# Reading and inverting most softmax denominators before two attentions end, and a reordered ScalarE loop in the first projection

## The chip, the cores and the metric

One core of a Trainium2 chip runs the whole program: TensorE (PE, matrix products), VectorE (DVE), ScalarE (ACT), GpSimd (POOL) and SyncE (SP, which here only issues DMAs). Each engine follows its own instruction list, and they meet through semaphores. The metric is the device time of one execution in microseconds, lower is better.

## The reference

The program is four layers over 8 sequences of 512 tokens with 128 features. Each layer adds an attention-like stage and then a mixture of experts. Only two stages are touched, the attentions of layers 0 and 1. Both have 16 heads of 8 features. Cut to what matters:

```python
# layer 0: 16 query heads, 8 key heads, and a memory read beside the attention
scores = einsum('bsnd,btnd->bnst', q4, k4) * scale
a_dot = einsum('bnst,btnd->bsnd', softmax(scores), v4)
a_mem = (elu(q) @ memory) / (elu(q) @ memory_norm)[..., None]
x = x + a_dot * (1 - w) + a_mem * w
# layer 1: the same with 16 key heads and a causal mask; q, k, v come from three "pattentions"
o = causal_sdpa(q, k, v)
```

The 8 sequences are called chunks here (NB = 8, L = 512 columns each, x is kept transposed as 128 features by 4096 tokens).

## The kernel before

The stages a0 (layer 0's attention), f0 (its experts), a1, f1, a2 and so on follow each other. Each stage is one or more blocks: an instruction list per engine, with a barrier of all engines between two blocks, so a block starts when the last engine has left the one before.

**The projection of layer 0** (`layer0_project`) loops over the chunks. Per chunk PE makes denominators and numerators of the memory read, projects q, k and v of the chunk two ahead, counts squares of up to three weight tiles ("jobs": the weight norms of f0, 17 jobs in all, spread over chunks 1 to 6; `count_squares`), and then spreads the inverted denominators over the rows (`spread_inverse`, L1366). ACT per chunk moves q, k and v out of PSUM with their variants, squares the job tiles (L1447, which wait in turn for PE to have counted earlier jobs), copies the numerators of the chunk before (`copy_num`, L1411) and widens its inverted denominators (`widen`, L1417). PE's `spread_inverse` of that chunk waits for `widen`.

**The attention** (`attend`) works a chunk at a time in 8 waves, half of a chunk behind its own score tiles (BEHIND = 4). For every group of 4 heads the maxima go through a short chain: DVE reduces, POOL splits them in three parts, PE turns them, DVE copies them to SBUF, POOL stores the 12 KB rows to DRAM (L1040), waits for them to land, and loads them back as rows of the operand `a_q` (L1043); the score products of that group wait for this. The products with v, whose 9th row of each head is the softmax denominator, are evacuated by ACT (L1164) and stored by SP as `a_pv_rows` (L947), 256 KB per group of 4 heads. Two operand buffers alternate: chunk 6 uses buffer 0, chunk 7 buffer 1. SP's block ends after the last store has landed.

**The division** (`combine`, a block of its own after the attention) loads all 128 denominator rows (L1557), inverts them on DVE (L1584), builds a 0/1 matrix `a_pick` on POOL (L1566, L1569), and for each chunk spreads the inverses with one f32 product of PE (L1579, two MATMUL instructions) and multiplies the numerators with them (L1590 in layer 1; L1592 and L1595, which also weighs and adds into x, in layer 0). The numerators are loaded 256 KB at a time into four buffers (L1561).

Of the kernel before, what the change touches and what calls it, by code (L numbers as in the profile page):

```python
# [12 lines left out]
F32 = mybir.dt.float32  # L13
# [850 lines left out]
def attend(nc, S, a):  # L864
# [7 lines left out]
    s, KVH, HK = S.at, a.KVH, H // a.KVH  # L872
    call = s.calls
    s.calls += 1
    with ExitStack() as ctx:
# [61 lines left out]
        def _(sp):  # L937
# [44 lines left out]
            for b in range(1, NB):  # L982
                body(b, True, True, b % 2)
            body(NB, False, True, 0)
            for k in range(2):
                sp.wait_ge(s.pv_stored[k], 16 * 2 * (nB + NB))

        @block.gpsimd
        def _(pool):
# [56 lines left out]
            steps(pool, body)  # L1046

# [133 lines left out]
        def _(dve):  # L1181
# [25 lines left out]
            steps(dve, body)  # L1207
    if a.causal:
        s.causal += 1
# [34 lines left out]
def layer0_attention(nc, S, inp, f):  # L1244
# [23 lines left out]
    attend(nc, S, a)  # L1268
    held.close()
    combine(nc, S, a, S.x, S.w_dot[:, 0:1])  # L1270


def layer0_project(nc, S, a, w, f):
# [19 lines left out]
    def jobs_of(c):  # L1293

        return range(min(3 * (c - 1), JOBS), min(3 * c, JOBS)) if c >= 1 else range(0)

    with ExitStack() as ctx:
# [105 lines left out]
        def _(act):  # L1403
# [16 lines left out]
            for c in range(NB):  # L1420
# [119 lines left out]

def combine(nc, S, a, dst, weight=None):

    sem, nm = S.sem, a.name
    den_loaded, inverse, picked = sem(f"{nm}_den_loaded"), sem(f"{nm}_inverse"), sem(f"{nm}_picked")
    num_loaded = [sem(f"{nm}_num_loaded{k}") for k in range(4)]
    spread, multiplied = sem(f"{nm}_spread"), sem(f"{nm}_multiplied")
    with ExitStack() as ctx:
        num = ctx.enter_context(nc.sbuf_tensor(f"{nm}_num", [P, 4, L], F32))
        den = ctx.enter_context(nc.sbuf_tensor(f"{nm}_den", [P, L], F32))
        pick = ctx.enter_context(nc.sbuf_tensor(f"{nm}_pick", [P, NB, P], F32))  # L1550
        inv = ctx.enter_context(nc.psum_tensor(f"{nm}_inv", [P, 4, L], F32))
        rows = a.pv.rearrange("b g (j r) n -> (b g j) r n", j=4)
        block = ctx.enter_context(nc.Block())

        @block.sync
        def _(sp):
            sp.dma_start(den[:, :], rows[:, DH, :]).then_inc(den_loaded, 16)  # L1557
            for b in range(NB):
                if b >= 4:
                    sp.wait_ge(multiplied, b - 3)  # L1560
                sp.dma_start(num[:, b % 4, :], rows[H * b:H * b + H, 0:DH, :]).then_inc(num_loaded[b % 4], 16)  # L1561

        @block.gpsimd
        def _(pool):

            nc.gpsimd.memset(pick[:, :, :], 0.0).then_inc(picked, 1)  # L1566
            pool.wait_ge(picked, 1)
            view = pick[:, :, :].rearrange("k b (h d) -> k (b h) d", d=DH)
            nc.gpsimd.affine_select(out=view, in_=view, compare_op=ALU.not_equal, fill=1.0, base=0,  # L1569
                                    pattern=[[-1, P], [0, DH]], channel_multiplier=1).then_inc(picked, 1)  # L1570

        @block.tensor
        def _(pe):
            pe.wait_ge(picked, 2)
            pe.wait_ge(inverse, 1)
            for b in range(NB):
                if b >= 4:
                    pe.wait_ge(multiplied, b - 3)
                nc.tensor.matmul(inv[:, b % 4, :], pick[:, b, :], den[:, :], start=True, stop=True).then_inc(spread, 1)  # L1579

        @block.vector
        def _(dve):
            dve.wait_ge(den_loaded, 16)
            nc.vector.reciprocal(den[:, :], den[:, :]).then_inc(inverse, 1)  # L1584
            for b in range(NB):
                dve.wait_ge(num_loaded[b % 4], 16 * (b // 4 + 1))
                dve.wait_ge(spread, b + 1)
                to = dst[:, b * L:(b + 1) * L]
                if weight is None:
                    nc.vector.tensor_tensor(to, num[:, b % 4, :], inv[:, b % 4, :], ALU.mult).then_inc(multiplied, 1)  # L1590
                else:
                    nc.vector.tensor_tensor(num[:, b % 4, :], num[:, b % 4, :], inv[:, b % 4, :], ALU.mult  # L1592
                                            ).then_inc(inverse, 1)
                    dve.wait_ge(inverse, b + 2)
                    nc.vector.scalar_tensor_tensor(out=to, in0=num[:, b % 4, :], scalar=weight, in1=to,  # L1595
                                                   op0=ALU.mult, op1=ALU.add).then_inc(multiplied, 1)
# [271 lines left out]
def layer1_attention(nc, S, inp):  # L1868
# [3 lines left out]
    with ExitStack() as ctx:  # L1872
# [23 lines left out]
        attend(nc, S, a)  # L1896
        held.close()
        combine(nc, S, a, g)
# [1144 lines left out]
```

## Time and profile before

| | us |
|---|---|
| median of 3 runs (lowest to highest) | 3603.91 (3601.78 to 3606.88) |
| the profiled execution | 3613.86 |
| its span, first to last instruction | 3612.1 |
| PE busy | 3240.8 (90% of the span) |
| DVE busy | 2450.0 (68%) |
| ACT busy | 1820.7 (50%) |
| POOL busy | 1191.2 (33%) |
| mean granted PE clock, as a share of 2.4 GHz | 0.926 |

The profile is of one execution that took 3613.86 us. Its span leaves out 1.8 us around the first and the last instruction. Busy shares are means over stages that have different limits, so the change is read in the three short stretches that it touches.

### The profile page before, as it was taken

What the parts mean: (1) busy time and instruction counts of PE and PEld (TensorE: products, weight loads), DVE (VectorE), ACT (ScalarE), POOL (GpSimd) and SP (SyncE); (2) the same over time, 40 slices, a digit from 0 to 9 for tenths busy, and PEclk for the clock granted to TensorE, in tenths of its full rate; (3) what the DMA queues carried; (4) which work ended last, traced back from release to release, by engine and by line L of the source; (5) the groups of instructions that cost most, each with busy time, mean ns of one, the idle gap of its engine ahead of it and who ended that gap; (6) DMA issues with size and microseconds to landing.
All of it is one profiled execution on the core that took longest, in us unless ns stands there. A gap on an engine that the chain in (4) does not pass through costs nothing. (4 is left out here: it accounts for less than half of the span.)

```text
span 3612.1 us, 39566 instructions
## 1 busy us (share of the span) xinstructions
PE 3240.8 (90%) x12845; PEld 1536.3 (43%) x12845; DVE 2450.0 (68%) x4164; ACT 1820.7 (50%) x2881; POOL 1191.2 (33%) x1010
## 2 busy tenths in 40 slices
PE   8899998999997699979998789898898789889999
PEld 5422224444444354535544233333333354764443
DVE  4788874443338577746544899999999955656544
ACT  5366672444446355534333777777777633312221
POOL 4211110000002222210000799999999910210000
PEclk7699998999998799989899899999999979889999
DMA  4222201000002533110000443443443410000000
GB/s 129 66 69 65 61 31 33 1 0 1 1 19 81 132 88 91 60 39 1 1 1 25 153 153 147 148 157 144 155 152 147 147 45 3 1 1 1 0 1 24
DMA packets 113335, 232.14 MB, mean 64 GB/s; under 512 B 27701, under 2 KB 82378, under 8 KB 95754
## 3 DMA queue, kind: packets, MB, share of 16 engines
q1 hardware_dynamic: 109034, 228.02, 19.0%
q0 software_dynamic: 4096, 1.59, 0.2%
q8 instruction: 104, 1.70, 0.2%
q14 instruction: 101, 0.83, 0.1%
HBM read 191.46 MB, written 34.87 MB: 63 GB/s over the span
## 5 line engine op out<-in xcount | busy, mean ns | idle before, releaser
L1199 DVE TENSOR_REDUCE a_top<-a_sc 128x1 f32<-128x512 f32 (+3 forms) x1024 | 547.2, 584 | 162.3 <-PE a_sc L1075 102.5
L2406 POOL TENSOR_TENSOR a_g<-a_g,a_spread 128x1024 f32<-128x1024 f32 x255 | 597.7, 2363 | 41.4 <-DVE a_g L2336 40.8
L2336 DVE TENSOR_TENSOR_SCAN a_g<-a_decay,a_drive 128x512 f32<-128x512 f32 x510 | 587.1, 1201 | 16.3 <-ACT a_drive L2225 12.9
L1156 ACT ACTIVATE a_prob<-a_st 128x1024 f32<-128x1024 f32 (+2 forms) x512 | 422.5, 862 | 280.7 <-PE a_st L1092 182.9
L705 DVE TENSOR_TENSOR f_s<-f_a,f_spread 128x512 f32<-128x512 f32 x392 | 269.4, 687 | 381.8 <-PE f_y L547 170.6
L2084 PE MATMUL a_y<-a_g,ident 128*128 128x512 f32 x1024 | 481.0, 610 | 31.3 <-POOL a_g L2406 31.3
L538 PE MATMUL f_hid<-h,f_w 128*128 128x512 f32 x784 | 404.2, 597 | 0.0
L547 PE MATMUL f_y<-f_s,f_w 128*128 128x512 f32 x784 | 401.6, 594 | 2.6 <-DVE f_s L705 2.6
L2209 ACT ACTIVATE a_decay<-a_delta,a_capped_a 128x512 f32<-128x512 f32 x512 | 331.8, 710 | 12.4 <-DVE a_g L2336 9.7
L1072 PE MATMUL a_sc<-a_k,a_q 96*128 96x512 bf16 (+3 forms) x1024 | 311.4, 357 | 20.9 <-POOL a_mask_k L996 11.2
L2084 PEld LDWEIGHTS a_y<-a_g,ident 128*128 128x128 f32 x1024 | 198.4, 197 | 306.7 <-issue 246.1
L602 ACT ACTIVATE f_a<-f_hid,f_b,f_norms 128x512 f32<-128x512 f32 x256 | 198.8, 777 | 255.2 <-PE f_hid L538 255.2
L1089 PE MATMUL a_st<-a_q,a_k 128*128 128x512 bf16 (+3 forms) x1024 | 284.0, 346 | 29.9 <-DMA a_q<-a_max_rows 28.2
L1107 PE MATMUL a_pv<-a_prob,a_v 128*32 128x512 f32 (+3 forms) x2048 | 234.7, 527 | 0.6 <-ACT a_prob L1156 0.3
L620 POOL CAST f_gates_f<-f_gates_b 96x512 f32<-96x512 bf16 x24 | 14.7, 612 | 653.6 <-ACT f_gates_b L583 653.6
L547 PEld LDWEIGHTS f_y<-f_s,f_w 128*128 128x128 f32 x784 | 146.4, 189 | 196.4 <-issue 177.5
L2380 POOL TENSOR_TENSOR a_pd<-a_du_s,a_spread 128x1024 f32<-128x1024 f32 x96 | 227.2, 2366 | 0.1
L602 ACT ACTIVATE f_a<-f_hid 128x512 f32<-128x512 f32 x136 | 81.2, 597 | 289.6 <-PE f_hid L535 289.6
L753 DVE TENSOR_TENSOR f_m<-f_a,f_hid 128x512 f32<-128x512 f32 x136 | 93.6, 688 | 181.0 <-ACT f_a L602 180.6
L538 PEld LDWEIGHTS f_hid<-h,f_w 128*128 128x128 f32 x784 | 148.0, 191 | 158.0 <-issue 151.7
L2325 DVE TENSOR_TENSOR a_drive<-a_du,a_spread 128x512 f32<-128x512 f32 x320 | 203.6, 682 | 0.0
L1089 PEld LDWEIGHTS a_st<-a_q,a_k 128*128 128x128 bf16 x1024 | 86.9, 98 | 252.4 <-ACT a_prob L1156 114.6
(396 smaller groups left out, 4903.0 us busy)
## 6 DMA issues: line engine op xcount, KB each, us to landing
a_spread<-a_bc_rows SPq DMA_DIRECT2D x128, 1024.0 KB, 4.6
a_q<-a_q_rows SPq DMA_DIRECT2D x192, 96.0 KB
a_pv_rows<-a_pv_sb SPq DMA_DIRECT2D x48, 256.0 KB, 2.0
a_k<-a_k_rows SPq DMA_DIRECT2D x288, 32.0 KB
a_k<-a_k_rows SPq DMA_DIRECT2D x288, 16.0 KB
a_num<-a_pv_rows SPq DMA_DIRECT2D x16, 256.0 KB, 3.6
a_pv_rows<-a1q_vf SPq DMA_DIRECT2D x16, 256.0 KB, 2.1
a_q_rows<-p_qp SPq DMA_DIRECT2D x24, 128.0 KB
```

Of the source, the lines that this page charges most:

```text
L538: nc.tensor.matmul(hid[:, n % 4, :], unit.w1, h[:, chunk(c)], start=True, stop=True).then_inc(f.hidden, 1)
L547: nc.tensor.matmul(y[:, :], f.units[u].w2, s[:, (n - LAG) % R, :], start=(u == 0), stop=(u == U - 1 and f.b2 is None)).then_inc(f.used, 1)
L602: nc.scalar.activation(a[:, n % R, :], hid[:, slot, :], f.func, bias=unit.bias if unit.bias is not None else 0.0, scale=unit.scale if unit ...
L705: nc.vector.tensor_tensor(s[:, n % R, :], (m if gated else a)[:, n % R, :], spread[:, k % 2, :], ALU.mult).then_inc(f.scaled, 1)
L1072: last = nc.tensor.matmul(sc[:, at % 3, 0:w], q[k][0:MAX_AT, n, t * P:(t + 1) * P], kk[k][0:MAX_AT, n // HK, 0:w], start=True, stop=not a. ...
L1089: last = nc.tensor.matmul(st[:, j % 2, col:col + wide], kk[k][:, n // HK, key:key + P], q[k][:, n, first:first + wide], start=True, stop=n ...
L1156: nc.scalar.activation(prob[w % 2][:, j, 0:width(kp)], st[:, j % 2, 0:width(kp)], ACT.Exp, scale=a.scale).then_inc(s.exp_done, 1)
L1199: nc.vector.tensor_reduce(top[:, t, n:n + 1], sc[:, slot(4 * n + t) % 3, 0:w], AX.X, ALU.max).then_inc(s.maxed, 1)
L2084: last = nc.tensor.matmul(y[:, k, :], S.ident[:, :], g[:, n % 8, k, :], start=False, stop=(n == STATES - 1))
L2209: last = nc.scalar.activation(decay[:, n % 4, k, :], delta[:, d, k, :], ACT.Exp, scale=capped_a[d][:, k, n:n + 1])
L2336: nc.vector.tensor_tensor_scan(to, decay[:, n % 4, k, way], drive[:, k, way], 0.0, ALU.mult, ALU.add).then_inc(scanned, 1)
L2406: nc.gpsimd.tensor_tensor(g[:, n % 8, :, :], g[:, n % 8, :, :], spread[:, pair % 4, 2 + n % 2:3 + n % 2, :].to_broadcast([P, H2, L]), ALU. ...
```

## The change

It has two parts. (The change's name speaks of a scan as well; no line of the scan stage, `layer2_mamba`, differs.)

First, in both attentions, the division's beginning moves into the attention's block. After the store of chunk 7's first group SP loads the denominators of chunks 0 to 6 (112 rows) and the numerators of chunks 0 to 3 into operand buffer 0, which chunk 6 was the last to use. DVE inverts the 112 rows at the end of its list, POOL builds the 0/1 matrices at the end of its own. SP no longer waits for the last stores inside the attention's block; that wait opens the division's block, followed by four small loads of chunk 7's 16 denominator rows. DVE inverts these (128x128) ahead of chunk 5's product, and chunk 7's spreading is done by four products of 128 columns with a second 0/1 matrix. The tiles `den`, `num` and `pick` are now parts of the operand buffers `a_q` and `a_k`, and carry these names in the listings.

Second, in the first layer's projection, ACT copies the numerators and widens the inverses ahead of the squares.

```diff
@@ attend, SP @@
             for b in range(1, NB):
                 body(b, True, True, b % 2)
+            sp.wait_ge(s.st_done, (nB + NB - 1) * 32)
+            for k in range(2):
+                sp.wait_ge(s.pv_stored[k], 16 * 2 * (nB + NB - 1))
+            sp.dma_start(m.den[0:EARLY, :], m.rows[0:EARLY, DH, :]).then_inc(m.den_loaded, 16)
+            for b in range(4):
+                sp.dma_start(m.num[:, b, :], m.rows[H * b:H * b + H, 0:DH, :]).then_inc(m.num_loaded[b], 16)
             body(NB, False, True, 0)
-            for k in range(2):
-                sp.wait_ge(s.pv_stored[k], 16 * 2 * (nB + NB))
+            a.pv_landed = [(s.pv_stored[k], 16 * 2 * (nB + NB)) for k in range(2)]
@@ attend, POOL @@
             steps(pool, body)
+            pool.wait_ge(s.st_done, (nB + NB - 1) * 32)
+            build_picks(nc, pool, m)
@@ attend, DVE @@
             steps(dve, body)
+            dve.wait_ge(m.den_loaded, 16)
+            nc.vector.reciprocal(m.den[0:EARLY, :], m.den[0:EARLY, :]).then_inc(m.inverse, 1)
@@ layer0_project, ACT @@
+                if c >= 1:
+                    copy_num(c - 1)
+                    widen(c - 1)
                 for n in jobs_of(c):
                     if n == 0:
                         act.wait_ge(f.loaded, 16 * f.n_loads)
                     if n >= 3:
                         act.wait_ge(counted, n - 2)
                     nc.scalar.activation(sq[n % 3][:, 0:jobs[n].shape[1]], jobs[n], ACT.Square).then_inc(squared, 1)
-                if c >= 1:
-                    copy_num(c - 1)
-                    widen(c - 1)
@@ new @@
+EARLY = H * (NB - 1)
+def build_picks(nc, pool, m):
+    nc.gpsimd.memset(m.pick, 0.0).then_inc(m.picked, 1)
+    nc.gpsimd.memset(m.pick_last, 0.0).then_inc(m.picked, 1)
+    nc.gpsimd.memset(m.den_last, 1.0).then_inc(m.picked, 1)
+    pool.wait_ge(m.picked, 3)
+    view = m.pick.rearrange("k b (h d) -> k (b h) d", d=DH)
+    nc.gpsimd.affine_select(out=view, in_=view, compare_op=ALU.not_equal, fill=1.0, base=0,
+                            pattern=[[-1, P], [0, DH]], channel_multiplier=1).then_inc(m.picked, 1)
...
@@ combine @@
         def _(sp):
-            sp.dma_start(den[:, :], rows[:, DH, :]).then_inc(den_loaded, 16)
-            for b in range(NB):
-                if b >= 4:
-                    sp.wait_ge(multiplied, b - 3)
...
+            for landed, value in a.pv_landed:
+                sp.wait_ge(landed, value)
+            sp.wait_ge(m.picked, 5)
+            for q in range(4):
+                sp.dma_start(m.den_last[32 * q:32 * q + H, :], m.rows[EARLY:EARLY + H, DH, q * P:(q + 1) * P]
+                             ).then_inc(m.last_loaded, 16)
+            for b in range(4, NB):
+                sp.wait_ge(m.multiplied, b - 3)
+                sp.dma_start(m.num[:, b % 4, :], m.rows[H * b:H * b + H, 0:DH, :]).then_inc(m.num_loaded[b % 4], 16)
...
+            pe.wait_ge(m.picked, 5)
+            pe.wait_ge(m.inverse, 1)
...
+                else:
+                    pe.wait_ge(m.last_inverse, 1)
+                    for q in range(4):
+                        last = nc.tensor.matmul(inv[:, b % 4, q * P:(q + 1) * P], m.pick_last[:, q, :], m.den_last,
+                                                start=True, stop=True)
...
+                if b == 5:
+                    dve.wait_ge(m.last_loaded, 64)
+                    nc.vector.reciprocal(m.den_last, m.den_last).then_inc(m.last_inverse, 1)
```

What stood at the end of SP's list in layer 0's attention and at the start of its division, before (`a_pv_sb` is the evacuated product, `a_pv_rows` its place in DRAM; the first row gathers the attention's last nine stores):

```order
L947 DMA a_pv_rows<-a_pv_sb 128x512 x9
L1557 DMA a_den<-a_pv_rows 128x512
L1561 DMA a_num<-a_pv_rows 128x1x512 x8
```

And in the changed kernel:

```order
L948 DMA a_pv_rows<-a_pv_sb 128x512 x6
L988 DMA a_q<-a_pv_rows 112x512
L990 DMA a_q<-a_pv_rows 128x1x512 x4
L948 DMA a_pv_rows<-a_pv_sb 128x512 x3
L1598 DMA a_k<-a_pv_rows 16x128 x4
L1602 DMA a_q<-a_pv_rows 128x1x512 x4
```

The load of the denominators and four of the numerators' loads have moved ahead of chunk 7's last three stores.

ACT's list in the projection, from the end of one chunk to the end of the next, before (`p_sq` the squares, `p_num_f` the copied numerators, `p_inv_w` the widened inverses; m0_wn_summed counts PE's counted jobs):

```order
L1441 ACTIVATE p_v<-p_v_ps 128x256 [waits pj_projected]
L1447 ACTIVATE p_sq<-f_w 128x512 [waits m0_wn_summed] x3
L1411 ACTIVATE p_num_f<-p_num 128x512 [waits m0_merged,m0_num]
L1417 ACTIVATE p_inv_w<-p_inv_t 128x512 [waits m0_spread,m0_inverted]
L1424 ACTIVATE p_q<-p_qk_ps 128x512 [waits pj_q_parts,pj_projected]
```

And in the changed kernel:

```order
L1451 ACTIVATE p_v<-p_v_ps 128x256 [waits pj_projected]
L1421 ACTIVATE p_num_f<-p_num 128x512 [waits m0_merged,m0_num]
L1427 ACTIVATE p_inv_w<-p_inv_t 128x512 [waits m0_spread,m0_inverted]
L1460 ACTIVATE p_sq<-f_w 128x512 [waits m0_wn_summed] x3
L1434 ACTIVATE p_q<-p_qk_ps 128x512 [waits pj_q_parts,pj_projected]
```

The squares now stand behind the two activations that PE's spreading waits for, not ahead of them.

## Rows read from the trace of the kernel before

**Rows 1.** Windows: projection, first attention, its division (columns: PE, PEld, DVE, ACT, POOL, PEclk).
```profile
52.00:138.00 86.00, 73.71 (x324) 57.47 (x323) 48.30 (x66) 41.67 (x77) 21.51 (x20) 0.64 0.27 73
138.00:550.00 412.00, 404.16 (x2176) 113.58 (x2174) 336.35 (x544) 270.67 (x289) 76.04 (x236) 0.97 0.20 58
550.00:573.00 23.00, 9.41 (x16) 3.87 (x16) 14.32 (x17) 0.00 (x0) 2.94 (x3) 0.72 0.40 114
```

**Rows 2.** Timeline of layer 0's division: start, duration, instruction, idle before and releaser.
```profile
549.86 0.32 SPq L947 DMA_DIRECT2D a_pv_rows<-a_pv_sb  x1
552.84 0.32 SPq L1557 DMA_DIRECT2D a_den<-a_pv_rows  x1
...
555.58 3.35 DVE L1584 RECIPROCAL a_den<-a_den 128x512 f32<-128x512 f32 x1 [22.56 <-DMA a_den<-a_pv_rows]
...
559.08 9.41 PE L1579 MATMUL a_inv<-a_den,a_pick 128*128 128x512 f32 x16 [10.28 <-DVE a_den L1584]
...
561.23 0.69 DVE L1592 TENSOR_TENSOR a_num<-a_num,a_inv 128x512 f32<-128x512 f32 x1 [2.30 <-PE a_inv L1579]
...
571.97 0.75 DVE L1595 SCALAR_TENSOR_TENSOR x<-a_num,w_dot,x 128x512 f32<-128x512 f32 x1
573.00 2.66 POOL L612 MEMSET f_parts<- 128x3072 bf16 x1 [17.06 <-POOLq L1547]
```

**Rows 3.** Timeline of layer 1's division.
```profile
1558.68 0.32 SPq L947 DMA_DIRECT2D a_pv_rows<-a1q_vf  x1
1561.15 0.32 SPq L1557 DMA_DIRECT2D a_den<-a_pv_rows  x1
...
1575.19 0.69 DVE L1590 TENSOR_TENSOR a_g<-a_num,a_inv 128x512 f32<-128x512 f32 x1 [0.78 <-DMA a_num<-a_pv_rows]
...
1577.11 0.69 DVE L1590 TENSOR_TENSOR a_g<-a_num,a_inv 128x512 f32<-128x512 f32 x1 [0.16 <-DMA a_num<-a_pv_rows]
1578.17 1.17 POOL L1683 COPY a1p_h<-a_g 128x512 f32<-128x512 f32 x2 [13.92 <-SPq L1632]
```

**Rows 4.** Timeline of the projection, PE and then ACT.
```profile
85.02 1.09 PE L1378 MATMUL p_sums<-ones,p_sq 128*128 128x1 f32 x8
87.83 2.08 PE L1366 MATMUL p_spread<-ident,p_inv_w 128*128 128x128 f32 x8 [1.72 <-ACT p_inv_w L1417]
...
114.25 2.08 PE L1366 MATMUL p_spread<-ident,p_inv_w 128*128 128x128 f32 x8
...
119.53 1.71 PE L1378 MATMUL p_sums<-ones,p_sq 128*128 128x1 f32 x8
...
84.30 0.63 ACT L1447 ACTIVATE p_sq<-f_w 128x512 f32<-128x512 f32 x1 [5.82 <-PE p_sums L1374]
...
87.16 0.62 ACT L1417 ACTIVATE p_inv_w<-p_inv_t 128x512 f32<-128x512 f32 x1
```

**Rows 5.** Windows: PE's clock in the projection and behind both attentions.
```profile
88.00:96.00 8.00, 8.00 (x22) 5.42 (x23) 5.92 (x8) 4.46 (x9) 3.43 (x3) 0.50 0.19 50
...
549.00:550.00 1.00, 0.00 (x0) 0.00 (x0) 0.00 (x0) 0.47 (x1) 0.00 (x0) 1.00 0.00 0
...
1558.00:1559.00 1.00, 0.00 (x0) 0.00 (x0) 0.00 (x0) 0.59 (x1) 0.00 (x0) 1.00 0.00 0
```

**Rows 6.** Timeline: POOL's 12 KB loads of the maxima, and PE behind one.
```profile
1215.87 0.52 POOL L1043 DMA_DIRECT2D a_q<-a_max_rows  x1 [6.35 <-DMA a_max_rows<-a1q_qp]
...
1547.45 0.52 POOL L1043 DMA_DIRECT2D a_q<-a_max_rows  x1 [1.67 <-DMA a_max_rows<-a1q_qp]
...
538.05 0.11 PEld L1089 LDWEIGHTS a_st<-a_q,a_k 128*128 128x128 bf16 x2 [0.88 <-DMA a_q<-a_max_rows]
...
1549.86 0.10 PEld L1089 LDWEIGHTS a_st<-a_q,a_k 128*128 128x128 bf16 x1 [0.74 <-DMA a_q<-a_max_rows]
```

**Rows 7.** A window with loads of 256 KB queued, and the page's list of DMAs.
```profile
555.60:559.00 3.40, 0.00 (x0) 0.00 (x0) 3.33 (x1) 0.00 (x0) 0.34 (x1) 0.50 0.89 251
...
a_num<-a_pv_rows SPq DMA_DIRECT2D x16, 256.0 KB, 3.6
```

More of the change, by code:

```diff
@@ L872, in attend @@
     s, KVH, HK = S.at, a.KVH, H // a.KVH
+    m = a.merge = combine_buffers(S, a)
     call = s.calls
@@ L1538, in _, with combine_buffers @@
             scale_w2(1)
+def combine_buffers(S, a):
+    m = State()
+    sem, nm = S.sem, a.name
+    m.den_loaded, m.inverse, m.picked = sem(f"{nm}_den_loaded"), sem(f"{nm}_inverse"), sem(f"{nm}_picked")
+    m.last_loaded, m.last_inverse = sem(f"{nm}_last_loaded"), sem(f"{nm}_last_inverse")
+    m.num_loaded = [sem(f"{nm}_num_loaded{k}") for k in range(4)]
+    m.spread, m.multiplied = sem(f"{nm}_spread"), sem(f"{nm}_multiplied")
+    m.den = a.q[:, 0:2, :].bitcast(F32).rearrange("p a n -> p (a n)")
+    m.num = a.q[:, 2:10, :].bitcast(F32).rearrange("p (c a) n -> p c (a n)", a=2)
+    m.pick = a.q[:, 10:14, :].bitcast(F32).rearrange("p a (u d) -> p (a u) d", d=P)
+    m.pick_last = a.k[:, 0:2, :].bitcast(F32).rearrange("p a (u d) -> p (a u) d", d=P)
+    m.den_last = a.k[:, 2, 0:2 * P].bitcast(F32)
+    m.rows = a.pv.rearrange("b g (j r) n -> (b g j) r n", j=4)
+    return m
@@ L1541, in combine @@
 def combine(nc, S, a, dst, weight=None):
[L1543 to L1546, printed above, removed]
+    m = a.merge
     with ExitStack() as ctx:
[L1548 to L1552, printed above, removed]
+        inv = ctx.enter_context(nc.psum_tensor(f"{a.name}_inv", [P, 4, L], F32))
@@ L1558, in _ @@
+        @block.tensor
+        def _(pe):
+            pe.wait_ge(m.picked, 5)
+            pe.wait_ge(m.inverse, 1)
             for b in range(NB):
                 if b >= 4:
-                    sp.wait_ge(multiplied, b - 3)
[L1561 to L1575, printed above, removed]
-            for b in range(NB):
-                if b >= 4:
-                    pe.wait_ge(multiplied, b - 3)
-                nc.tensor.matmul(inv[:, b % 4, :], pick[:, b, :], den[:, :], start=True, stop=True).then_inc(spread, 1)
+                    pe.wait_ge(m.multiplied, b - 3)
+                if b < NB - 1:
+                    last = nc.tensor.matmul(inv[:, b % 4, :], m.pick[0:EARLY, b, :], m.den[0:EARLY, :],
+                                            start=True, stop=True)
[3 more added lines that the diff above has]
+                        last = nc.tensor.matmul(inv[:, b % 4, q * P:(q + 1) * P], m.pick_last[:, q, :], m.den_last,
+                                                start=True, stop=True)
@@ L1581, in _ @@
+                last.then_inc(m.spread, 1)
         @block.vector
         def _(dve):
-            dve.wait_ge(den_loaded, 16)
-            nc.vector.reciprocal(den[:, :], den[:, :]).then_inc(inverse, 1)
             for b in range(NB):
-                dve.wait_ge(num_loaded[b % 4], 16 * (b // 4 + 1))
-                dve.wait_ge(spread, b + 1)
+                if b == 5:
+                    dve.wait_ge(m.last_loaded, 64)
+                    nc.vector.reciprocal(m.den_last, m.den_last).then_inc(m.last_inverse, 1)
@@ L1896, in layer1_attention @@
         attend(nc, S, a)
+        combine(nc, S, a, g)
         held.close()
-        combine(nc, S, a, g)
         def merge_inner(dve, c, y):
```

19 lines of the change are left out of this document (12 added, 7 removed).

## The prediction

> **What bounds the kernel now.** I read the windows by stage first, then the timeline of the stretches that the change touches. In the projection PE is busy 73.71 of 86 us, at a mean granted clock of 0.64; in the first attention 404.16 of 412 us at 0.97 [rows 1]. So both are PE's, and in both what makes PE wait or slows its start counts in full. The division is different: of 23 us PE works 9.41 and DVE 14.32, ACT nothing [rows 1]. It is a chain: in layer 0 SP issues the last store at 549.86, the denominators' load follows at 552.84 (store landed, barrier), the reciprocal runs from 555.58 for 3.35 us, PE starts at 559.08, DVE's first product at 561.23, its last instruction ends at 571.97 + 0.75 = 572.72, and the next stage starts at 573.00 [rows 2]. The reader is to see that from 549.86 to 561.23, 11.4 us, no engine does anything that needs chunk 7, except the small part of the reciprocal. Layer 1 has the same shape: last store at 1558.68, last product done at 1577.11 + 0.69 = 1577.80, next stage at 1578.17 [rows 3].
>
> In the projection the row to look at is PE's spreading at 87.83, which waited 1.72 us for ACT's widening; ACT had begun it at 87.16, behind the squares, the first of which at 84.30 had waited 5.82 us for PE's counts [rows 4]. That gap of 1.72 us comes four times in the timeline (at 59.23, 73.69, 87.83 and 101.95).
>
> **The division of layer 0.** After the last store's issue (549.86 + 0.32) the block ends without waiting for the landing. The barrier costs 0.28 us (572.72 to 573.00 [rows 2]), so PE can start at about 550.5: the inverses and the 0/1 matrices were made while the attention's last waves ran. From PE's start to DVE's first product took 2.15 us, at the lower clock of 1.2 GHz: 9.41 us for 16 MATMULs begins with two of them at some 0.86 us [rows 2]. Here PE was busy until just before, and the granted clock at 549 to 550 is still 1.00, that is 2.4 GHz [rows 5]; I halve the two MATMULs (1.72 to 0.86) and keep the other 0.43: 1.3 us. First product at 551.8. From first product to the end DVE needed 572.72 - 561.23 = 11.49 us; with no cold first products I take 11.2. New on DVE's path is the reciprocal of 128x128, a quarter of 3.35, 0.85 us. Its bounds are 0.85 and, if fixed cost dominated, 3.35; the row scales with columns elsewhere (0.69 for 512), so 0.85. Chunk 7's four products (8 MATMULs of 128 columns) lie under DVE's two chunks before it: 2.08 us for such eight at the lower clock [rows 4] against 2 x 1.44. End at 551.8 + 11.2 + 0.85 = 563.9 instead of 572.7: **8.8 us less**. Moved SP work: the wait for the landing (2.98 us between store and next issue with a barrier [rows 2]), four small issues at 0.35, so chunk 4's numerators are issued at about 554.1 and land 3.6 us later [rows 7] at 557.7; DVE wants them at 551.8 + 4 x 1.39 = 557.4. That is 0.3 us at most, taken as part of the range.
>
> **The division of layer 1.** The last store is issued at 1558.68, PE starts at 1559.3, first product at 1560.6. Products 0 to 3 follow PE's pace of 0.86 us to 1563.9. The chunk 7 store has landed by 1561.15 less a barrier of 0.3 [rows 3]; four issues later, at 1562.3, chunk 4's numerators are issued and land 3.3 us later at 1565.6 (DVE already waits on these loads before: 0.78 us at 1575.19 [rows 3]). Product 4 to 1566.3, reciprocal to 1567.15, products 5 and 6 to 1568.6, chunk 7's spreading (1567.2 plus 1.04, half of 2.08, plus 0.3) is ready then, product 7 to 1569.3. Against 1577.8: **8.5 us less**. Here SP's four small issues do cost, some 1.4 us, which is in the sum.
>
> **What the early loads collide with.** SP issues 224 KB of denominators and 4 x 256 KB behind the store of chunk 7's first group, at 534.96 in layer 0 (store at 534.6) and 1537.7 in layer 1. At 251 GB/s [rows 7] 1.25 MB keep the DMA engines busy for 5 us. POOL's load of the last group's maxima is issued at 535.9 in layer 0, in the middle of it, and PE takes up its products at 538.05, with the weight load already 0.88 us idle behind that landing [rows 6]: there is no slack, and each us later is a us of the attention. In layer 1 the load of the third group (issued 1538.0) is hit; the last group's, issued 1547.45, is behind the backlog, and PE waits 0.74 us for it at 1549.86 [rows 6], which absorbs 0.74 us of the lateness. The bounds of the delay: nothing, and what the largest hit in the trace shows, POOL idle 6.35 us instead of 1.67 for a 12 KB landing, 4.7 us more [rows 6]. That one stood behind 448 KB copies that were issued within 6 us; the traffic here is about as much but in 2 KB rows. I take 1.8 us for the landing: **1.8 lost in layer 0, 1.0 in layer 1.** The Trainium skill ("DMA: Bandwidth & Descriptors", section Queues, rings and completion order) says that each DMA engine takes its queues in turn, a packet at a time, typically 9 to 17 descriptors. By it POOL's load would wait for one share of a 256 KB load and no more, an estimate of 1.0 us (256 KB at the row's 251 GB/s) for each of its steps, and the sum would be 1 us better; the 4.7 us of the row speak against so short a wait.
>
> **The projection.** With the widening ahead of the squares PE finds it done when the counts end. The 1.72 us go four times, 6.9 us. The new wait: in chunk 1 ACT now waits for DVE's first inversion with three squares queued behind it, about 0.3 us. In the later chunks widening waits for PE's denominators, done before its q, k and v of two ahead, so ACT has idle time to spare (5.82 us before the first square [rows 4]). Does the clock follow? PE ran 88 to 96 at 0.50 without a gap, and the spreading at 114.25, which followed the counts with no idle, also took 2.08 us, as the one at 87.83 behind a gap [rows 4, 5]. So the counts alone bring PE back to 1.2 GHz, and I expect no gain of clock: **6.6 us less**. POOL's two fills and two selects and DVE's 3.4 us reciprocal in the attention are hidden: after their last work both idle over 13 us in either layer (22.56 us for DVE, which includes the old load [rows 2]).
>
> **Sum.** 8.8 + 8.5 + 6.6 - 1.8 - 1.0 = 21.1 us. The profiled execution's 3613.86 becomes 3592.8. It stood 0.28% above the median, so against the median 3603.91 I forecast 3582.8, rounded 3583.
>
> **Rivals.** (a) *The landing is hit as hard as the hardest row.* 4.7 and 4.7 - 0.74 instead of 1.8 and 1.0: 5.9 us more, 3589. For it: the backlog is of the same size; against: most other landings in the attention with SP's loads about are under 1 us late. (b) *The clock stays up in the projection.* Without the gap the lower stretch (88 to 96, 8 us that would be about 4 to 5) shrinks, until ACT's own chain of a chunk limits it: 2.7 us more in four chunks, 3572. Against it stands the row at 114.25. (c) *The reordering gives nothing*: the counts drift into the lower clock (1.71 us for eight instead of 1.09 [rows 4], 1.9 us a chunk), which pays the gap back: 3590. (d) *The block's end still waits for the stores in flight*, so the change doesn't free the start: 2.2 us in each layer, 3587. Nothing in the profile shows either. (e) *Slower.* The early loads hold up POOL's load of the maxima so long that the attention loses more than all gains, 23.9 us before collisions: it needs over 12 us in each layer, from a landing of 2 us to over 14. It decides from there; at 14.5 each the kernel would take 3609. The largest landing in the trace is under 7.
>
> **How the numbers follow.** The forecast has 0.58, with its own range from 3578 to 3588; (a) 0.14, (b) 0.11, (c) 0.09, (d) 0.06, (e) 0.02. From 3574 to 3591 holds the forecast, (a), (c) and (d), and the upper part of (b). 0.2% is 7.2 us, about what a measurement tells from no change; every case but (e) is faster by more than 10 us, and I leave 0.03 for mixtures that end within it: faster 0.95, same 0.03, slower 0.02.
>
> **What the profile after would show.** PE's first product of each division within 1.5 us of SP's last store, at 1.00 clock, and DVE's first 1.3 us behind it; from last store to next stage 14.1 us in layer 0 (was 23.1) and 11.0 in layer 1 (was 19.5). A gap before chunk 7's product, or over 1 us before chunk 4's in layer 0, would prove the SP part wrong. PE's wait for `a_q<-a_max_rows` near chunk 7's last groups should grow from 0.88 to about 2.7 us; above 5 it is (a). The projection's spreadings should show no idle behind `p_inv_w`, still at about 2 us each. Wrong altogether would be an attention longer by more than 10 us, or a projection no shorter.

## The result, and the profile after

| | before | changed |
|---|---|---|
| median of 4 runs | 3605.39 us | 3575.44 us |
| lowest to highest | 3601.78 to 3614.10 | 3570.72 to 3580.96 |
| profiled execution (span) | 3613.86 (3612.1) | 3580.96 (3579.2) |
| mean granted clock | 0.926 | 0.931 |

The ratio of the changed kernel to the one before is 0.9914, with a 95% interval from 0.9890 to 0.9937: 30 us less by the medians, and from 23 to 40 by the interval. The same file, timed again in a later set of runs (e7 below), gave 0.9915 (0.9898 to 0.9933). The forecast was 3583 with a range from 3574 to 3591.

Where did the time go? I read the windows of the three stages first. These are the windows of the changed kernel from the first spreading of the projection to the attention's first score matmul, from there to the end of the last store's issue, and from there to the next stage; the columns are those of [rows 1].

```profile
48.31:125.25 76.94, 70.75 (x343) 54.73 (x342) 45.48 (x68) 45.30 (x84) 22.03 (x20) 0.69 0.32 86
125.25:536.40 411.15, 396.79 (x2136) 113.54 (x2176) 339.21 (x545) 270.59 (x289) 80.56 (x241) 0.97 0.21 62
536.40:550.45 14.05, 8.56 (x22) 4.27 (x22) 11.69 (x17) 0.00 (x0) 0.00 (x1) 0.83 0.34 96
```

The first row is the projection, the second the attention, the third the division. The division is down from 23 us to 14, the attention is as long as before.

The projection needs another look, since [rows 1] cut it elsewhere. The same cut in the kernel before:

```profile
49.46:137.88 88.42, 76.13 (x342) 59.59 (x342) 49.77 (x68) 44.18 (x82) 21.39 (x20) 0.65 0.28 75
```

The reader is to see two differences of like size. PE's idle time fell from 88.42 - 76.13 = 12.29 us to 76.94 - 70.75 = 6.19, that is 6.1 us. And PE's busy time fell by 5.4 us for the same matmuls, at a mean granted clock of 0.69 instead of 0.65. The forecast had the first and denied the second. The timeline of PE and ACT in the changed kernel shows the first (answer to [rows 4]):

```profile
68.06 2.05 PE L1376 MATMUL p_spread<-ident,p_inv_w 128*128 128x128 f32 x8
...
79.21 1.14 PE L1376 MATMUL p_spread<-ident,p_inv_w 128*128 128x128 f32 x8
...
89.39 2.05 PE L1376 MATMUL p_spread<-ident,p_inv_w 128*128 128x128 f32 x8
...
66.35 0.63 ACT L1460 ACTIVATE p_sq<-f_w 128x512 f32<-128x512 f32 x1 [3.04 <-PE p_sums L1384]
```

No spreading waits for the widening any more, and ACT, whose first square waits 3.04 us for PE's counts (5.82 before), has taken the slack. The second of the three ran in 1.14 us, at the full clock (1.00), which none behind a gap did in the kernel before.

Layer 0's division (answer to [rows 2]), with SP, PE, DVE and the next stage's first instruction:

```profile
536.08 0.32 SPq L948 DMA_DIRECT2D a_pv_rows<-a_pv_sb  x1
536.99 6.63 PE L1612 MATMUL a_inv<-a_q 112*128 112x512 f32 x14 [1.67 <-PEq L876]
538.14 1.71 SPq L1598 DMA_DIRECT2D a_k<-a_pv_rows  x4
538.19 0.69 DVE L1633 TENSOR_TENSOR a_q<-a_q,a_inv 128x512 f32<-128x512 f32 x1 [15.48 <-PE a_inv L1612]
...
539.90 4.46 SPq L1602 DMA_DIRECT2D a_q<-a_pv_rows  x4
...
543.74 0.68 DVE L1633 TENSOR_TENSOR a_q<-a_q,a_inv 128x512 f32<-128x512 f32 x1
...
545.12 0.95 DVE L1626 RECIPROCAL a_k<-a_k 128x128 f32<-128x128 f32 x1
...
549.42 0.75 DVE L1636 SCALAR_TENSOR_TENSOR x<-a_q,w_dot,x 128x512 f32<-128x512 f32 x1
550.45 2.66 POOL L612 MEMSET f_parts<- 128x3072 bf16 x1 [22.87 <-POOLq L1588]
```

PE starts 0.91 us after the store, DVE 1.20 us after PE, and from there DVE doesn't stop until 550.17: no row of it has an idle time, not even chunk 4's first product at 543.74. Last store to next stage: 14.37 us. Layer 1 (answer to [rows 3]):

```profile
1534.23 0.32 SPq L948 DMA_DIRECT2D a_pv_rows<-a1q_vf  x1
1535.15 6.25 PE L1612 MATMUL a_inv<-a_q 112*128 112x512 f32 x14 [1.67 <-PEq L876]
1536.35 0.69 DVE L1631 TENSOR_TENSOR a_g<-a_q,a_inv 128x512 f32<-128x512 f32 x1 [12.95 <-PE a_inv L1612]
...
1538.05 2.45 SPq L1602 DMA_DIRECT2D a_q<-a_pv_rows  x4
...
1541.48 0.69 DVE L1631 TENSOR_TENSOR a_g<-a_q,a_inv 128x512 f32<-128x512 f32 x1 [1.87 <-DMA a_q<-a_pv_rows]
...
1545.48 0.61 POOL L1724 COPY a1p_h<-a_g 128x512 f32<-128x512 f32 x1 [17.20 <-SPq L1673]
```

Here the first products pace with PE, one in 0.86 us, and chunk 4's waits 1.87 us for numerators that SP could issue no earlier than 1538.05. Last store to next stage: 11.25 us. The clock behind both last stores is 1.00, as in [rows 5]:

```profile
536.00:537.00 1.00, 0.01 (x1) 0.04 (x1) 0.00 (x0) 0.00 (x0) 0.00 (x0) 1.00 0.11 39
...
1534.00:1535.00 1.00, 0.00 (x0) 0.00 (x0) 0.00 (x0) 0.14 (x1) 0.00 (x0) 1.00 0.00 0
```

The last look is at what the early loads hit. This is SP with POOL and PE in layer 0's chunk 7 (answer to [rows 6]):

```profile
511.27 0.34 SPq L988 DMA_DIRECT2D a_q<-a_pv_rows  x1
511.66 2.74 SPq L990 DMA_DIRECT2D a_q<-a_pv_rows  x4
...
522.31 0.52 POOL L1049 DMA_DIRECT2D a_q<-a_max_rows  x1 [1.68 <-DMA a_max_rows<-a_max_row]
...
524.57 0.55 PEld L1097 LDWEIGHTS a_st<-a_q,a_k 128*128 128x128 bf16 x4 [0.97 <-DMA a_q<-a_max_rows]
```

The loads go out 11 us ahead of POOL's last load, not beside it, and the wait of PE's weight load behind it is 0.97 us instead of 0.88.

I cut all profiles at the same milestones; the table is in us and worked out from the timelines. "Middle" is from layer 0's division to the start of layer 1's attention (SP's first copy of its head tensors), the divisions run from the last store's issue to the next stage, and the attentions up to that store. "Rest" is from layer 1's division to the end; the stretch ahead of the projection's first spreading (49.46 us before, 48.31 in the changed kernel) is in no column.

| kernel | projection | attention 0 | division 0 | middle | attention 1 | division 1 | rest |
|---|---|---|---|---|---|---|---|
| before | 88.42 | 411.98 | 23.14 | 629.68 | 356.00 | 19.49 | 2033.93 |
| changed | 76.94 | 410.83 | 14.37 | 633.07 | 350.71 | 11.25 | 2033.72 |
| e1 order only | 77.64 | 411.69 | 23.23 | 629.11 | 345.78 | 19.71 | 2031.29 |
| e2 divisions only | 87.97 | 411.53 | 14.37 | 630.90 | 350.52 | 11.28 | 2031.71 |
| e3 gap filled | 84.77 | 411.61 | 23.10 | 629.57 | 353.06 | 19.51 | 2035.23 |
| e4 end waits | 80.36 | 410.40 | 17.30 | 630.53 | 347.37 | 13.08 | 2032.60 |
| e5 all early | 76.81 | 413.13 | 14.38 | 630.87 | 344.11 | 9.55 | 2034.89 |
| e6 beside last maxima | 77.14 | 412.79 | 14.38 | 630.84 | 347.29 | 11.21 | 2035.04 |
| e7 changed again | 76.78 | 411.57 | 14.38 | 628.42 | 337.82 | 11.09 | 2031.07 |
| e8 counts twice | 108.21 | 411.46 | 14.38 | 628.38 | 345.04 | 11.59 | 2032.76 |
| e9 wide counts | 66.79 | 411.66 | 14.38 | 628.30 | 347.45 | 11.31 | 2031.05 |
| e10 wide, old order | 72.34 | 411.62 | 23.34 | 628.17 | 354.92 | 20.31 | 2034.15 |
| e11 best | 66.87 | 411.75 | 14.39 | 628.10 | 342.73 | 9.55 | 2030.96 |

Between before and changed the span fell by 32.9 us: 1.2 ahead of the projection's first spreading, 11.5 projection, 1.2 attention 0, 8.8 division 0, minus 3.4 middle, 5.3 attention 1, 8.2 division 1, 0.2 rest. The change touches work that is worth 11.5 + 8.8 + 8.2 = 28.5 of it.

### The profile page after: what moved, and what is told of

Its sections match the earlier page's. It is cut to its first block and busy times, and to the rows that moved or that the text cites. A ratio compares the mean times of both kernels' runs of the same rounds, so it can differ in the third digit from the quotient of the medians.

```text
span 3579.2 us, 39538 instructions
## 1 busy us (share of the span) xinstructions
PE 3218.7 (90%) x12785; PEld 1534.2 (43%) x12857; DVE 2445.3 (68%) x4166; ACT 1821.4 (51%) x2881; POOL 1194.1 (33%) x1016
## 5 line engine op out<-in xcount | busy, mean ns | idle before, releaser
L1097 PE MATMUL a_st<-a_q,a_k 128*128 128x512 bf16 (+1 forms) x952 | 264.3, 341 | 10.3 <-issue 5.9
```

The source lines that it names most:

```text
L1097: last = nc.tensor.matmul(st[:, j % 2, col:col + wide], kk[k][:, n // HK, key:key + P], q[k][:, n, first:first + wide], start=True, stop=n ...
```

## Experiments

**e1_order_only: the kernel before with ACT's new order alone.**

```diff
+                if c >= 1:
+                    copy_num(c - 1)
+                    widen(c - 1)
                 for n in jobs_of(c):
...
-                if c >= 1:
-                    copy_num(c - 1)
-                    widen(c - 1)
```

> The kernel before with ScalarE's new order in layer 0's projection and nothing else. Theory: the order alone gave the whole 12.6 us (11.3 net of an earlier start) that the projection is shorter by in the changed kernel, half of it idle time of PE (6.1 us) and half clock (PE busy 5.9 us less for the same 354 matmuls). So from 45 us to the attention's first score matmul PE's idle time falls by about 6 us and its busy time by about 6, the stage ends about 11 us earlier, both divisions stay at 23.1 and 19.5 us from last store to next stage, and the kernel takes 0.25 to 0.35% less than before. Rival (my forecast's step): only the gaps go, the busy time stays at 80.7 us, 6.6 us or 0.18% less, and the other 5 us came from somewhere else in the changed kernel.

Measured: ratio 0.9981 (0.9970 to 0.9993), 7 us less; in its profile the projection is 77.64 us (88.42 before). The window of that stage, columns as above:

```profile
47.55:125.19 77.64, 72.13 (x343) 56.57 (x342) 45.48 (x68) 45.29 (x84) 21.98 (x20) 0.69 0.32 86
```

Idle 5.5 us, 6.8 less than before, and busy 4.0 less. So the order alone gives both halves; the stage's 10.8 us are inside the timed interval (0.07 to 0.30%) at its far end, and 7 us is the better guess of the kernel's gain.

**e2_divisions_only: the changed kernel with the old order** (the edit above, backwards).

> The changed kernel with ScalarE's old order in the projection. Theory: the two divisions are worth 8.8 and 8.2 us wherever the clock's phases fall; 14.4 and 11.3 us from last store to next stage, PE idle and busy in the projection as before (four gaps of 1.72 us), attention of layer 0 and of layer 1 not longer than before. Kernel about 17 us or 0.47% less than before. Rival: part of the 32 us came by the phases of the clock, which the two parts share, so that this one alone gives under 12 us or over 22.

Measured: ratio 0.9941 (0.9923 to 0.9959), 21 us less. Both divisions repeat to 0.03 us (14.37, 11.28), the projection is the old one (87.97, four gaps of 1.72). The stages give 17.0 us, inside the interval of 15 to 28. With e1 the two ratios add up to 0.78%, the changed kernel has 0.86%: no sign of an interaction that these timings could show.

**e3_gap_filled: PE has work in the gap.** The kernel before with

```diff
             def spread_inverse(c):
+                if 1 <= c <= 4:
+                    for t in range(3):
+                        nc.tensor.matmul(filler[:, t * P:(t + 1) * P], S.ident[:, :], S.ident[:, :],
+                                         start=True, stop=True)
                 pe.wait_ge(widened, c + 1)
...
```

> The kernel before, with its old order, and three extra 128x128 products of the identity (six matmuls into a bank that nobody reads) ahead of each of the four spreadings that waited for ScalarE: PE has work in the gap, and the spreading can begin no earlier than before. Theory (the idle gap is what lowers the clock behind it): the stretches of 0.50 shrink, PE's busy time for the other work falls by 3 us or more, and the kernel is 2 to 6 us faster than before though it does more. Rival (the gap is not what sets the clock; the narrow counts or the phase of the chunk are): the lower stretches stay at about 10 us each, the added products take 1.6 us each in the place of the gap, and the kernel takes the same or up to 2 us more.

Measured: ratio 0.9991 (0.9979 to 1.0004), which can't be told from none. The projection is 84.77 us, 3.65 shorter, but the distances of the spreadings are 9.77, 14.24, 10.82, 14.10, 12.23, 7.25 and 9.79 us against 9.77, 14.46, 14.14, 14.12, 12.30, 7.27 and 9.79 before: one chunk of four gained, the others next to nothing. The gap is mostly filled but not gone: PE still waits 0.87, 0.33, 0.23 and 0.23 us for the widening. So filling most of the gap held the clock in one chunk of four only; that the gap alone sets it is not borne out. Neither theory predicted this shape.

**e4_end_waits: SP waits for the last stores within the attention again.**

```diff
-            a.pv_landed = [(s.pv_stored[k], 16 * 2 * (nB + NB)) for k in range(2)]
+            a.pv_landed = []
+            for k in range(2):
+                sp.wait_ge(s.pv_stored[k], 16 * 2 * (nB + NB))
```

> The changed kernel, except that SP again waits within the attention for the landing of the last stores, so the block and with it the division can't begin before. Theory: the landing and the barrier take about 2.5 us, PE's first product of a division comes 3 us after the last store instead of 0.9, the clock is still 1.00, and each division is 2 to 2.5 us longer in layer 0; in layer 1, where the late loads set the end, 0 to 1 us longer, since SP's late loads are issued at the same time as before. Kernel about 2.5 to 3 us (0.08%) slower than the changed one. Rival: PE's pause lowers the clock, then the first products take 0.86 us each and the cost is 4 us a layer.

Measured: 2.9 us more in layer 0's division, 1.8 in layer 1's (rival (d) had 2.2 each); ratio to before 0.9925 (0.9909 to 0.9941), some 4 us above the changed kernel, which the timing alone can't tell from none. PE's start, from the timeline, and a window just behind it:

```profile
541.30 7.08 PE L1614 MATMUL a_inv<-a_q 112*128 112x512 f32 x12 [3.43 <-PEq L876]
```

```profile
542.00:544.00 2.00, 2.00 (x4) 0.77 (x3) 0.64 (x1) 0.00 (x0) 0.00 (x0) 0.50 0.07 17
```

PE starts 2.68 us after the store instead of 0.91, and behind 3.43 us of idle time the clock is 0.50, so DVE's first product comes 2.07 us after PE's start instead of 1.20. Starting at once saves the wait and keeps the clock. My theory had the clock at 1.00 and only 0 to 1 us in layer 1; the rival had the clock right and, at 4 us a layer, its price too high.

**e5_all_early: seven numerators before the last store instead of four.** Three more buffers, and in SP's list

```diff
-            for b in range(4):
-                sp.dma_start(m.num[:, b, :], m.rows[H * b:H * b + H, 0:DH, :]).then_inc(m.num_loaded[b], 16)
+            for b in range(NB - 1):
+                sp.dma_start(m.num[b], m.rows[H * b:H * b + H, 0:DH, :]).then_inc(m.num_loaded[0], 16)
...
```

> The changed kernel, with the numerators of all seven finished chunks loaded early (three more buffers in the freed head tensors), so that after the last store SP fetches only chunk 7's denominators and numerators. Theory (DVE sets layer 0's division, the late numerators layer 1's; early traffic costs nothing): layer 0's division stays at 14.4 us, in layer 1 the wait of 1.87 us before chunk 4's product is gone and last store to next stage is 9.9 instead of 11.25 us; 2 MB instead of 1.25 MB early makes neither attention longer. Kernel 0 to 1.5 us less than the changed one. Rival (my forecast's collision, now with 8 us of backlog): POOL's landings are later, each attention 1 to 3 us longer, and the kernel slower than the changed one by 1 to 4 us.

Measured: 0.9918 (0.9900 to 0.9936), not to be told from the changed kernel. Both theories hold, each in its place: layer 1's division is 9.55 us (1.7 less, the wait is gone), and the attention pays 1.6 us in layer 0 (413.13 against 411.57 in e7, on the same chip; the builds without a load near the last maxima have 410.40 to 411.98). The wait for the last maxima in layer 0 shows it:

```profile
527.89 0.55 PEld L1097 LDWEIGHTS a_st<-a_q,a_k 128*128 128x128 bf16 x4 [2.20 <-DMA a_q<-a_max_rows]
```

It was 0.97; in layer 1 it went from 0.75 to 1.94. What that costs layer 1's attention can't be read, since this stage varies by more (e7 below).

**e6_beside_last_maxima: the early loads where the forecast thought they were.**

```diff
+            sp.wait_ge(s.evacuated, (nB + NB - 1) * 4 + 1 + 3)
             sp.dma_start(m.den[0:EARLY, :], m.rows[0:EARLY, DH, :]).then_inc(m.den_loaded, 16)
```

> The changed kernel, with the five early loads issued one store later, when chunk 7's second group is evacuated: about 1.2 us before POOL issues the load of the last group's maxima, which PE takes up with no slack. This is the collision that my forecast priced, put where it was thought to be. Theory (the two queues share the DMA engines, a 12 KB landing grows little): PE's wait for the last maxima grows by under 1 us, layer 0's attention stays within 1 us of 411, layer 1's as well. Rival 1 (my forecast's term): 1.8 us longer in layer 0, 1.0 in layer 1. Rival 2 (the landing waits for the whole backlog of 5 us): 3.5 to 4.7 us longer in each.

Measured: 0.9922 (0.9906 to 0.9938). SP issues at 521.85 (which also pushes its own store of chunk 7's second group to 525.09), POOL's last load follows at 523.12, and PE's weight load waits for it at

```profile
526.53 0.55 PEld L1098 LDWEIGHTS a_st<-a_q,a_k 128*128 128x128 bf16 x4 [2.13 <-DMA a_q<-a_max_rows]
```

1.2 us more, and attention 0 is 1.2 us longer than in e7: between my theory (under 1 us) and the forecast's term (1.8). In layer 1 the wait grew from 0.75 to 1.14 only. The Trainium skill ("DMA: Bandwidth & Descriptors", section Queues, rings and completion order) says that a DMA engine takes its queues in turn, packet by packet; the forecast's estimate by it was 1.0 us a step, and the trace's 1.2 us in layer 0 is near it, the 0.4 in layer 1 is below it, and the 4.7 of [rows 6] is far off. That turns by packet are the cause is not shown by these waits.

**e7_changed_again.** The changed kernel, unedited.

> The changed kernel once more, to see what of its profile repeats. Theory: the divisions (14.4 and 11.2 us) and layer 0's attention (411) repeat to 0.2 us; the projection (76.9 us), the long stage between the attentions (633) and layer 1's attention vary by some us with the phase of the clock, so that the 32.9 us between the two profiled spans hold about 5 us of chance. Kernel 0.7 to 0.9% less than before. Rival: the profile repeats throughout, and the 4.3 us by which layer 1's attention is shorter belong to the change.

Measured: 0.9915 (0.9898 to 0.9933). The profiled span is 3558.9 us, 20.3 less than that of the same kernel above: 12.9 of these lie in attention 1 (337.82 against 350.71), 4.7 in the middle, 2.7 in the rest. The divisions and the projection repeat to 0.2 us, attention 0 to 0.8. Even so a projection with the same instructions took 80.36 us in e4, 3.4 more than here. The 5.3 us that attention 1 seemed to gain and the 3.4 us that the middle seemed to lose are less than what the unedited kernel shows between two profiles, so neither can be put down to the change. Whether attention 1 gains a little stays open: it took 345.8 to 356.0 us in the four builds with the old division and 337.8 to 350.7 in the nine with the new one.

**e8_counts_twice: more one-column products, no idle time.** Every count of the squares (`p_sums`) in the changed kernel's projection is done twice, with the same result.

```diff
             def count_squares(n):
                 pe.wait_ge(squared, n + 1)
+                if n < E:
+                    for t in range(HT):
+                        nc.tensor.matmul(sums[:, n * HT + t:n * HT + t + 1], sq[n % 3][:, t * P:(t + 1) * P],
+                                         S.ones[:, 0:1], start=True, stop=True)
...
```

> The changed kernel with every count of the squares in the projection done twice on PE (24 more matmuls of one column in each of four chunks; the second overwrites the first with the same). PE still has no idle time ahead of its spreadings, but more time in which its products have one column. Theory (it was the idle gap that lowered the clock, the narrow products do not): the counts take 1.4 to 2.8 us more in each of four chunks and the rest of PE's work takes no longer than in the changed kernel; projection 6 to 11 us longer. Rival (narrow products lower the clock, as my forecast's step had it): on top of that the wide products run at 0.50 for longer, their busy time rises by 3 to 6 us, and the projection is 12 us longer or more.

Measured: 0.9997 (0.9985 to 1.0008), the whole gain of 30 us gone.

```profile
49.58:157.79 108.21, 102.70 (x470) 86.46 (x470) 44.87 (x68) 45.28 (x84) 21.51 (x20) 0.62 0.22 62
```

The stage is 31.4 us longer than in e7. The rows of `p_sums` grew from 17.0 to 48.6 us, nearly three times as much for twice the work, since more of them ran at 0.50; the sum of all other rows of PE grew from some 60 to 65 (66 before the change). My theory that idle time sets the clock falls: PE hardly stood still here, and the clock was lower than with the gaps. The price that I gave for the added counts (1.4 to 2.8 us a chunk) was too low by half; at 0.50, 24 of them take over 5 us.

**e9_wide_counts: the same counts with 128 columns.** The changed kernel with

```diff
-                        last = nc.tensor.matmul(sums[:, n * HT + t:n * HT + t + 1], sq[n % 3][:, t * P:(t + 1) * P],
-                                                S.ones[:, 0:1], start=True, stop=True)
+                        last = nc.tensor.matmul(sums[:, n * HT + t:n * HT + t + P], sq[n % 3][:, t * P:(t + 1) * P],
+                                                S.ones[:, :], start=True, stop=True)
...
```

> The changed kernel with every count of the squares done with 128 columns of ones instead of one; the same number of matmuls, the same sums in the first column, and the overwritten columns are never read. Theory (it is the stretch of one-column and two-column products that lowers the clock, the gap behind it only adds): 24 counts at full clock take about 3.1 us instead of 2.8, but the stretches of 0.50 become short or vanish, PE's busy time for the other products falls from 60 to 62 us (sum of their rows in the changed kernel and its repeat) to 45 to 52, the mean granted clock of the projection goes from 0.70 to over 0.85, and the stage is 5 to 12 us shorter than the 76.8 of the changed kernel; kernel 5 to 12 us faster than it. Rival (the narrow columns are not the cause; only idle time and the phase count): clock stays at 0.70, stage 1 to 4 us longer than 76.8, since 128 columns cost more than one at either clock.

Measured: 0.9883 (0.9868 to 0.9897), 3561.88 us, some 11 us less than the changed kernel. Its windows, the whole stage and then 30 us of it, and after them the same 30 us of the changed kernel:

```profile
47.56:114.35 66.79, 54.35 (x343) 42.18 (x343) 44.77 (x68) 44.95 (x84) 21.95 (x20) 0.95 0.37 99
...
60.00:90.00 30.00, 25.86 (x165) 19.42 (x166) 19.15 (x29) 24.50 (x47) 11.24 (x10) 1.00 0.46 126
```

```profile
60.00:90.00 30.00, 30.00 (x149) 22.08 (x148) 15.94 (x22) 20.11 (x38) 10.85 (x9) 0.73 0.42 114
```

PE is less busy and more is done: 165 matmuls in 25.86 us against 149 in 30.00. And the wide counts cost no more than the narrow ones, as two timeline rows at full clock show, of e9 and of the changed kernel:

```profile
62.65 2.90 PE L1384 MATMUL p_sums<-ones,p_sq 128*128 128x128 f32 x24
```

```profile
99.14 2.79 PE L1388 MATMUL p_sums<-ones,p_sq 128*128 128x1 f32 x24
```

**e10_wide_old_order: wide counts, and the gap left in.** The kernel before with e9's edit.

> The kernel before with the same wide counts, and ScalarE's old order. PE still has to wait for ScalarE ahead of four spreadings, the longer the faster PE is: gap without narrow counts. Theory (narrow counts lower the clock): the clock stays at 1.00 for most of the stage although the gap is there and grows from 1.72 to 2 us or more; the stage is 4 to 9 us shorter than the 88.4 of before. Rival (the idle gap lowers the clock): the stretches of 0.50 behind each gap stay at 7 to 10 us, and the stage is as long as before or up to 3 us longer.

Measured: 0.9960 (0.9947 to 0.9972); projection 72.34 us, 16.1 less than before, more than either theory had. A window of 30 us, and two of the four spreadings from the timeline, the third and the fourth, with a window behind the fourth:

```profile
60.00:90.00 30.00, 24.43 (x153) 18.05 (x153) 16.63 (x23) 21.62 (x41) 10.86 (x9) 1.00 0.41 114
```

```profile
78.81 1.16 PE L1366 MATMUL p_spread<-ident,p_inv_w 128*128 128x128 f32 x8 [1.72 <-ACT p_inv_w L1417]
...
89.20 1.16 PE L1366 MATMUL p_spread<-ident,p_inv_w 128*128 128x128 f32 x8 [1.72 <-ACT p_inv_w L1417]
```

```profile
92.00:94.00 2.00, 2.00 (x3) 0.67 (x2) 1.84 (x4) 1.96 (x5) 0.20 (x1) 0.50 0.39 115
```

The four gaps of 1.72 us are there. The clock stays at 1.00 behind the first three; behind the fourth the spreading still runs in 1.16 us, but from 92 to 94 us the clock is 0.50. So it is the one-column counts that bring the clock down in every chunk: with them widened, and nothing else changed, the stage's mean goes from 0.65 to 0.94. A gap of this size doesn't do it by itself in three cases of four; whether it plays a part in the fourth is open, as it is in e9, where the clock falls once too, at 101 us, behind idle times of 1.58 and 0.42 us. e10 to e9 is also the order's worth with the clock nearly held (0.94 and 0.95): 72.34 - 66.79 = 5.6 us.

**e11_best: all together.** Wide counts, e5's seven early numerators, but the last three behind chunk 7's third store:

```diff
+            early(range(4))
+            store(NB - 1, 1)
+            store(NB - 1, 2)
+            early(range(4, NB - 1))
+            store(NB - 1, 3)
...
```

> Wide counts, ScalarE's new order, and the divisions with all numerators of the finished chunks early: four behind chunk 7's first store as in the changed kernel, the other three behind its third store, when POOL has no load of maxima left to hit. Theory: PE's last wait for the maxima is 0.9 us again (it was 2.2 where all seven were loaded at once), both attentions as long as in the changed kernel, layer 1's division 9.6 us instead of 11.25, layer 0's 14.4, and the projection as in the run with wide counts: 7 to 14 us less than the changed kernel if wide counts help, 1.7 us less if they don't. Rival: the three late ones come too late or hold back chunk 7's own rows, the division of layer 1 stays at 11 us or more.

Measured: 0.9879 (0.9864 to 0.9894), 3560.85 us, the lowest of all. Layer 1's division is 9.55 us, PE's wait for the last maxima 0.91 (2.20 in e5), attention 0 411.75. The 1.8 us over e9 are in the profile; the timing alone couldn't tell the two apart.

## Why the prediction was right, and where it wasn't

**Division of layer 0** (forecast 8.8 us): 8.8. PE began 0.91 us after the store (forecast 0.6) at clock 1.00 and DVE 1.20 behind it (forecast 1.3), the reciprocal took 0.95 (0.85), chunk 4's numerators came in time. e2 and e7 repeat it.

**Division of layer 1** (8.5): 8.2. The step that SP's four small issues push chunk 4's numerators late was right: DVE waits 1.87 us for them, and e5 and e11, which load them early, are 1.7 us shorter.

**The early loads** (minus 1.8 and minus 1.0): nothing. The failed step is "SP issues ... behind the store of chunk 7's first group, at 534.96 in layer 0 (store at 534.6)". That store was the second group's; the first group's was at 524.4, as chunk 7's first two stores in the kernel before show:

```profile
524.38 0.32 SPq L947 DMA_DIRECT2D a_pv_rows<-a_pv_sb  x1
...
534.62 0.32 SPq L947 DMA_DIRECT2D a_pv_rows<-a_pv_sb  x1
```

So the loads were never in the middle of POOL's last load. They fell on the third group's, issued at 512.08 in the changed kernel, behind which PE's products don't wait. Put where I thought they were, they cost 1.2 us (e6) and the bigger load 1.6 (e5): the size was about right, the place was wrong. In layer 1 the place was right. PE's first product behind the third group's maxima now waits 0.53 us, but from chunk 7's first store to its last it is 21.31 us before and 21.32 after, and the wait for the last maxima is 0.75 us as before (0.74). That load was issued at 1523.0, 9.7 us behind the first early load, when by the forecast's own 5 us the backlog was over.

**The projection** (6.6): 11.5 in the two profiles. The gaps went as forecast, 6.1 us of idle time. The failed step is "the counts alone bring PE back to 1.2 GHz, and I expect no gain of clock". The first half is right, and e8 to e10 show it more strongly than the trace of before could. The inference is wrong: that the clock falls on the counts doesn't say for how long, and with the pace of a chunk changed the stretches at 0.50 became shorter, 5.4 us less busy time (between 2.1 in e4 and 6.7 in e7 in builds with the same order, so the stage's gain is 8.1 us in e4 and 11.6 in e7). Rival (b) had the direction; its price, 2.7 us in each of four chunks or 10.8, was twice what the clock gave, and its reason, that without the gap the clock stays up, is borne out by neither e3 nor e8. What sets the length of a stretch with narrow counts is not settled: filling most of the gap helped one chunk of four (e3).

**The rivals.** (a), a landing as late as the hardest row: e6 says no. (c), reordering gives nothing: e1 says no. (d), the block's end waits: e4 put it in, and its price was 2.9 and 1.8 us. (e), slower: no sign of it in any run.

Sum by the stages: 28.5 us instead of 21.1, and the timed 30. The range held, with 1.4 us to spare at its lower end (3575.44 against 3574): the divisions were forecast to 0.3 us by the right steps, and two wrong steps, 2.8 us for the early loads and 4.9 for the projection, both put the forecast too high. That the range reached down far enough was owed to rival (b), so for this part it was luck.

## What to carry to other kernels

An f32 matmul with one moving column took as long as one with 128 here, and a run of them took the clock from all that stood behind it: where the granted clock falls although PE doesn't stand still, look for narrow products and widen them before reordering anything. For work behind a long loop, keep its inputs loading ahead and let PE go over without a pause, since the pause costs once in time and once in clock. And place an issued transfer in the trace by the instruction it follows, counted from the list, before pricing what it collides with.

## What the hardware showed that I had not expected

- PE was busy 102.70 of 108.21 us at a mean granted clock of 0.62 in e8 and 54.35 of 66.79 us at 0.95 in e9; the kernels differ in how often the squares are counted and with how many columns. The Trainium skill ("TensorE: Matmul & The Clock Gate", section Why this matters for your kernels) advises to keep TensorE busy and free of idle gaps between bursts to hold the full clock. By it e8, with no idle ahead of its spreadings, should have held the full clock at least as well as e9; the measurement says the opposite, and it decides.
- 24 counts with one column took 2.79 us and with 128 columns 2.90, both at clock 1.00.
- A 12 KB load issued 1.3 us behind the first of five loads of 1.25 MB together made PE wait 1.2 us longer in layer 0 and 0.4 in layer 1 (e6), far from the 5 us that the backlog takes by my estimate from [rows 7].
- Two profiles of one kernel (changed and e7) differ by 20.3 us, 12.9 of them in layer 1's attention. The divisions and the projection repeat to 0.2 us in this pair, so a stage's own row says more than the difference of two spans. It takes more than one pair to know a stage, though: the same projection took 80.36 us in e4 and 76.78 to 77.14 in the changed kernel, e5, e6 and e7.
